# Third run of a four-step period in the order lists of an attention replaced by a list of its own to the attention's end

## The reference

```python
x = x + L0_xattn(ln(x), ctx)   # 16 heads of 128 in 4 groups, self and cross attention
x = x + L0_ffn(ln(x))          # 32 experts, top 8 of a softmax router, rerouted by similarity
x = x + L1_xattn(ln(x), ctx)   # latent attention with rotary parts and a mask
x = x + L1_ffn(ln(x))          # quantised gate, up and down projections
```

```python
q = ln(fp8_linear(ln_out, wq));  qx = ln(fp8_linear(ln_out, wqx))
k = ln(fp8_linear(ln_out, wk));  v = fp8_linear(ln_out, wv)
kx, vx = split(cond @ w_kv_x);   kx = ln(kx)
core = softmax(q k^T / sqrt(128)) v        # per batch and head, 256 x 256
xout = softmax(qx kx^T / sqrt(128)) vx     # per batch and head, 256 x 64
out = fp8_round(concat(core, xout) / proj_smooth) @ wproj.T * scale
```

## Time and profile before

| | before |
|---|---|
| median of three runs | 820.1 us (819.15 to 820.65) |
| profiled execution, own time | 821.01 us |
| its span | 819.2 us |
| PE busy | 776.4 us (95%) |
| DVE, ACT, POOL busy | 642.5, 538.4, 495.5 us |
| attention's last `project` (`add_o` follows) | 455.6 us |
| mean granted TensorE clock | 0.991 |

### The profile page before, as it was taken

How to read it: one execution, slowest core, us unless ns; L and a number is a source line. 1 busy time by engine, 2 the same in 40 slices (tenths; PEclk the granted TensorE clock), 3 DMA queues, 4 the chain that set the end, 5 groups by cost and what they waited for, 6 DMA issues and landing times.

```text
span 819.2 us, 14427 instructions
## 1 busy us (share of the span) xinstructions
PE 776.4 (95%) x4848; PEld 669.2 (82%) x4848; DVE 642.5 (78%) x1509; ACT 538.4 (66%) x1236; POOL 495.5 (60%) x858
## 2 busy tenths in 40 slices
PE   3678999999999999999899999999999999999997
PEld 2467888889888899888778878898888877777787
DVE  6878998989888898889889795766754658886644
ACT  6889878798787987788664555433332267986332
POOL 2698879997699976997856477424210125627410
PEclk9989999999999999999999999999999999999999
DMA  7000120012101030000200322977513000001001
GB/s 248 13 1 1 50 68 1 2 39 60 59 1 34 20 98 6 2 1 2 69 27 14 110 87 56 237 191 255 175 44 99 21 1 14 27 1 39 1 1 52
DMA packets 29224, 45.59 MB, mean 56 GB/s; under 512 B 4128, under 2 KB 18272, under 8 KB 29024
## 3 DMA queue, kind: packets, MB, share of 16 engines
q1 hardware_dynamic: 27760, 41.31, 17.0%
q10 hardware_dynamic: 1392, 3.37, 1.2%
HBM read 43.49 MB, written 1.18 MB: 55 GB/s over the span
## 4 chain that ended last, share of the span: by engine, by line
PE 81%; DVE 6%; ACT 6%; DMA 2%; issue 2%; POOL 2%; SPq 1%; ACTq 0%; DVEq 0%
PE PS L1077 17%; PE PS L937 10%; PE PS L1147 9%; PE PS L1032 6%; PE PS L968 6%; PE PS L1006 6%; PE PS L959 4%; PE PS L1261 3%; PE PS L978 3%; PE PS L989 3%; PE PS L1016 2%; PE PS L1213 2%; DMA l_S<-share 1%; PE PS L1223 1%; PE PS L1229 1%
## 5 line engine op out<-in xcount | busy, mean ns | idle before, releaser
L3240 POOL TENSOR_SCALAR raw<-raw,mvq,rsq 128x128 f32<-128x128 f32 x312 | 194.8, 638 | 1.6
L1077 PE MATMUL PS<-xq,WH 128*128 128x512 f32 x472 | 149.2, 397 | 0.0
L1077 PEld LDWEIGHTS PS<-xq,WH 128*128 128x128 f32 x472 | 86.3, 190 | 17.5 <-issue 1.9
L937 PE MATMUL PS<-WH,xq 128*128 128x256 f32 (+1 forms) x256 | 91.2, 373 | 9.9 <-DVE xq L2102 5.6
L1077 PE MATMUL PS<-xq,WL 128*128 128x512 f32 x236 | 92.9, 393 | 0.0
L937 PE MATMUL PS<-WL,xq 128*128 128x256 f32 (+1 forms) x256 | 83.3, 342 | 0.0
L2202 DVE BATCH_NORM_STATS2 st<-raw 128x6 f32<-128x128 f32 x320 | 75.3, 277 | 9.1 <-ACT raw L1398 7.7
L1147 PE MATMUL PS<-xq,m_hh 128*128 128x256 f32 x384 | 70.3, 283 | 2.0 <-ACT m_hh L1312 1.4
L1032 PE MATMUL PS<-PH,cat 128*128 128x256 f32 x256 | 67.8, 301 | 0.9 <-DVE cat L2102 0.9
L1426 ACT ACTIVATE P<-PS,sm 128x256 f32<-128x256 f32 x128 | 59.9, 483 | 13.1 <-DVE sm L2266 13.0
L1006 PE MATMUL PS<-PT,vr 128*128 128x256 f32 x256 | 66.3, 381 | 1.9 <-ACT kT L1415 1.4
(11 more groups left out here) (316 smaller groups left out, 2120.6 us busy)
## 6 DMA issues: line engine op xcount, KB each, us to landing
wst<-in_wgu SPq DMA_DIRECT2D x24, 256.0 KB, 2.9
wst<-in_wall SPq DMA_DIRECT2D x18, 256.0 KB, 3.1
l_KM<-share SPq DMA_DIRECT2D x9, 384.0 KB, 3.9
dst<-in_wdn SPq DMA_DIRECT2D x24, 128.0 KB, 2.6
wst<-in_wkvx SPq DMA_DIRECT2D x8, 256.0 KB, 3.4
m_pre<-in_wo ACTq DMA_DIRECT2D x1, 2048.0 KB, 11.7
l_KM<-share SPq DMA_DIRECT2D x6, 256.0 KB, 6.5
l_S<-share SPq DMA_DIRECT2D x6, 256.0 KB, 6.0
```

The costliest lines, as they stand in the source:

```text
L937: t = e.matmul(PS[:, b, o:o + n], xq[s][:, k, c * 128:(c + 1) * 128], W[:, k, w0:w0 + n], start=(k == 0 and i == 0), stop=(k == 1 and i == 1))
L1077: t = e.matmul(PS[:, b, :], W[wi][:, gu, k, :], a[:, k, cols], start=(n == 0), stop=(n == 5))
L3240: t = e.tensor_scalar(v, v, mvq[:, par, n, 0:1], rsq[:, par, n:n + 1], ALU.add, ALU.mult)
```

## The change

The loops of the period run twice instead of three times, and its `if g < 2` go. What the third run and the rule made is now a list of single calls on PE, ACT, DVE and POOL, with the same calls in another order. Four small pieces of code that stood between them got names (`split_gate`, `first`, `zero`, `turn_keys`) so that the lists can place them. Two waits moved into the functions that they guard: for `rounded` in POOL's `load_p` and in `load_gu`. The amount of work on each engine is as before.

```diff
 def attention_order(do):
-    for g in range(3):
+    for g in range(2):
...
-    units = [(s, k) for s in range(STEPS) for k in range(5)]
-    for n in range(BEGUN, len(units) + 5):
...
+    do("p1", 3, 7, 0)
+    do("project", 11, 2)
+    do("p1", 3, 6, 1)
+    do("p2", 14, 4)
...
+    do("project", 11, 3)
+    do("p2", 14, 0)
+    do("p1", 3, 7, 1)
+    do("values", 13, 0)
...
+    do("project", 12, 2)
+    do("project", 12, 3)
+    do("p2", 15, 4)
...
+    do("scores", 15, 2)
+    do("p2", 15, 3)
+    do("project", 13, 2)
+    do("xs", 0)
+    do("project", 13, 3)
+    do("values", 14, 3)
+    do("turn", 14, 4)
+    do("scores", 15, 3)
+    do("keys")
...
+    do("early", 0, 0)
+    do("project", 15, 0)
+    do("project", 15, 1)
+    do("early", 1, 0)
+    do("project", 15, 2)
+    do("project", 15, 3)
+    do("xs", 2)
+    do("logits", 1)
...
 def vector(e):
+            norm(14, 4)
+            split_x(0)
+            add_o(13)
+            maxima(15, 2)
+            split_gate()
+            ln_m(1)
...
 def gpsimd(e):
             def load_p(gp, p):
                 two = slice(2 * p, 2 * p + 2)
+                w.wait_ge(rounded.sem, rounded.at[12, 0])
...
+            norm_q(14, 5)
+            load_p(3, 2)
+            load_p(3, 3)
+            norm_q(14, 6)
+            norm_q(14, 7)
+            root_q(15)
...
+            norm_q(15, 7)
             norm_m(0)
+            load_gu(0)
+            zero()
+            load_gu(1)
             norm_m(1)
+            load_gu(2)
             load_dn(0)
             load_dn(1)
+            load_gu(3)
+            turn_keys()
```

More of the change, by code:

```diff
@@ L20 @@
 PARTS = (2, 0, 1)
-BEGUN = 73
 P2ORDER = (4, 0, 1, 2, 3)
@@ L310, in attention_order @@
         do("turn", 6 + 4 * g, 0)
-        if g < 2:
-            do("p1", 2 + g, 1, 1)
+        do("p1", 2 + g, 1, 1)
         do("p2", 7 + 4 * g, 0)
-    units = [(s, k) for s in range(STEPS) for k in range(5)]
-    for n in range(BEGUN, len(units) + 5):
[L316 to L350, removed]
@@ new lines, in attention_order @@
+    do("scores", 10, 3)
+    do("values", 10, 0)
+    do("turn", 10, 1)
+    do("p2", 11, 1)
+    do("kx", 3)
+    do("scores", 10, 4)
+    do("values", 10, 1)
+    do("turn", 10, 2)
+    do("p2", 11, 2)
+    do("p1", 3, 2, 2)
+    do("values", 10, 2)
+    do("turn", 10, 3)
+    do("scores", 11, 0)
+    do("p2", 11, 3)
+    do("p1", 3, 3, 2)
+    do("values", 10, 3)
+    do("scores", 11, 1)
+    do("turn", 10, 4)
+    do("project", 9, 0)
+    do("project", 9, 1)
+    do("p1", 3, 2, 0)
+    do("p1", 3, 3, 0)
@@ new lines, in attention_order @@
+    do("project", 9, 2)
+    do("scores", 11, 2)
+    do("p2", 12, 4)
+    do("scores", 11, 3)
+    do("values", 10, 4)
+    do("turn", 11, 0)
+    do("project", 9, 3)
+    do("p1", 3, 2, 1)
+    do("p1", 3, 3, 1)
+    do("p2", 12, 0)
+    do("values", 11, 0)
+    do("turn", 11, 1)
+    do("p1", 3, 4, 2)
+    do("scores", 11, 4)
+    do("p2", 12, 1)
+    do("values", 11, 1)
+    do("scores", 12, 0)
+    do("turn", 11, 2)
+    do("p2", 12, 2)
+    do("scores", 12, 1)
+    do("values", 11, 2)
+    do("turn", 11, 3)
@@ new lines, in attention_order @@
+    do("p2", 12, 3)
+    do("project", 10, 0)
+    do("p1", 3, 5, 2)
+    do("project", 10, 1)
+    do("p1", 3, 4, 0)
+    do("p1", 3, 5, 0)
+    do("values", 11, 3)
+    do("turn", 11, 4)
+    do("p1", 3, 4, 1)
+    do("project", 10, 2)
+    do("project", 10, 3)
+    do("p1", 3, 5, 1)
+    do("scores", 12, 2)
+    do("p2", 13, 4)
+    do("values", 11, 4)
+    do("scores", 12, 3)
+    do("turn", 12, 0)
+    do("p2", 13, 0)
+    do("kt", 3)
+    do("project", 11, 0)
+    do("values", 12, 0)
+    do("scores", 12, 4)
@@ new lines, in attention_order @@
+    do("scores", 14, 2)
+    do("turn", 13, 4)
+    do("project", 12, 2)
+    do("project", 12, 3)
+    do("p2", 15, 4)
+    do("scores", 14, 3)
+    do("values", 13, 4)
+    do("turn", 14, 0)
+    do("scores", 14, 4)
+    do("p2", 15, 0)
+    do("values", 14, 0)
+    do("turn", 14, 1)
+    do("project", 13, 0)
+    do("p2", 15, 1)
+    do("values", 14, 1)
+    do("scores", 15, 0)
+    do("turn", 14, 2)
+    do("p2", 15, 2)
+    do("project", 13, 1)
+    do("scores", 15, 1)
+    do("values", 14, 2)
@@ new lines, in attention_order @@
+    do("turn", 14, 3)
+    do("scores", 15, 2)
[7 more added lines that the diff above has]
+    do("keys")
+    do("values", 14, 4)
+    do("turn", 15, 0)
+    do("scores", 15, 4)
+    do("keys_r")
+    do("values", 15, 0)
+    do("turn", 15, 1)
+    do("logits", 0)
+    do("values", 15, 1)
+    do("turn", 15, 2)
+    do("project", 14, 0)
+    do("values", 15, 2)
+    do("turn", 15, 3)
@@ L353 @@
+    do("xs", 1)
+    do("project", 14, 1)
+    do("values", 15, 3)
+    do("turn", 15, 4)
+    do("project", 14, 2)
+    do("project", 14, 3)
+    do("values", 15, 4)
+    do("early", 0, 0)
[6 more added lines that the diff above has]
+    do("logits", 1)
 TAIL = 18
@@ L1751, in scalar @@
                 exps(6 + 4 * g, 2)
-                if g < 2:
-                    take_p1(2 + g, 0, 1)
+                take_p1(2 + g, 0, 1)
                 take_p2(7 + 4 * g, 0)
[L1755 to L1786, removed]
@@ L1788, in scalar @@
+            take_values(15, 4)
+            first(0)
+            first(1)
+            load_gu(3)
+            split_x(2)
             w.emptied(("o", STEPS - 1))
@@ L2772, in vector @@
+            go(y[30])
+            split_x(1)
+            go(y[30], 3)
+            add_o(14)
+            go(y[30])
+            go(y[31], 5)
+            ln_m(2)
+            add_o(15)
             w.emptied(("o", STEPS - 1))
```

558 lines of the change are left out of this document (462 added, 96 removed).

## The result

| | before | after |
|---|---|---|
| median | 820.1 us (5 runs, 819.0 to 820.78) | 814.5 us (5 runs, 811.53 to 816.26) |
| ratio after to before | | 0.9933, 95% interval 0.9908 to 0.9958 |
| profiled execution, span | 821.01, 819.2 us | 815.51, 813.7 us |
| PE idle from 388 to 446 us | 4.89 us | 0 |
| last values of the attention end | 444.63 | 438.52 |

The changed kernel is 5.6 us faster; 815.8 was forecast.

The account below looks back on a forecast made before the run. PE bounds up to 388 us; behind it order, not load, loses 7.1 us, 6.4 recoverable. Less 0.7 each for xs(0), xs(2) and small waits gives 4.3: median 815.8 from 820.1, range 813.8 to 819.3.

Parts of the forecast that it names:

- Up to 388 us: From 311 us PE has no wait to lose, so the new order brings 0, between -0.5 and +1 us of cost.
- wrong if PE waits in 311 to 388: Sign against the forecast: PE waiting between 311 and 388 us, a stretch that was to stay without a wait.
- The root of step 15: On POOL, it starts at 390.8 instead of 393.3, 2.5 us earlier, as its loads and seeds come sooner.
- project(12,2): PE's 0.9 us wait for `cat` goes: y[25] ends on DVE at 397.1, due about 397.8.
- `p2`(15,4): POOL's first pairs ready at 398.9, PE comes at 399.6; the waits for POOL, 1.3 us in sum, go.
- xs(0): xn ready at 416.1, PE there at 415.6: wait 0.5, with slower start 0.7, between 0 and 3 us.
- xs(2): Now directly behind project(15,3), PE waits between 0 and 0.9 us for ln_m(2); taken as 0.7.
- Small tenths: Less 0.7 us for waits left at tight places: project(12,2), the `l_KA` copy behind keys, turn(15,0).
- The gain carried to the end: From xs(2) on, router and experts do the same work behind the same logits, so the 4.3 us gain stays.
- The first rival: POOL's chain doesn't move, root at 393.3 or later; 1.2 to 2.5 us left, 817.6 to 818.9; chance 0.17.
- scores further ahead: Behind 388 us, 11.1 us of PE work instead of 6.2 from scores(15,4) to its transpose answers waits for `P` and ACT.
- about 0.9 shorter with none: POOL's root of step 15 runs about 0.9 us shorter if no DVE two-input instruction meets it, longer with one more.

Follow-up runs that it names:

- e2: Order of the kernel before up to about 388 us on PE, ACT, DVE and POOL, the changed kernel's order behind; 814.49 us beside 820.80, ratio 0.9933.
- e9: Changed kernel with DVE's last five seed steps for the root of step 15 moved behind maxima(13,4) alone; 817.26 us beside 820.34, ratio 0.9963.
- e5: Changed kernel with DVE's last five seed steps of step 15 behind maxima(13,4), a rounding pass and maxima(14,0); 820.19 us beside 820.48, ratio 1.0007.
- e3: Kernel before with transposes and values pushed one unit later behind unit 73, last roundings, projections and early halves too; 826.48 us beside 820.80, ratio 1.0095.
- e7: Kernel before with scores pulled one unit earlier on PE, exponentials on ACT, maxima and divisions on DVE; 822.65 us beside 820.48, ratio 1.0029.
- e6: Changed kernel's lists up to scores(15,0) at about 404 us (POOL's to the root of step 15), old order behind; 818.58 us beside 820.48, ratio 0.9970.
- e10: Changed kernel with DVE's five passes of each rounding y[26] to y[31] in one piece, nothing between them; 821.99 us beside 820.34, ratio 1.0018.
- e4: Order of the kernel before written as single calls in the changed kernel's code, with its moved waits for rounded; 820.37 us beside 820.80, ratio 0.9997.
- e11: Changed kernel with scores (15,1) to (15,4) one place later each on PE, exponentials, maxima and divisions moved along; 821.61 us beside 820.34, ratio 1.0008.
- e1: Changed kernel's lists up to about 388 us on all four engines, order of the kernel before behind; 820.01 us beside 820.80, ratio 0.9990.
- e8: Changed kernel with logits of batch 2 on PE ahead of the second early half instead of behind it; 817.07 us beside 820.48, ratio 0.9954.
- e12: Changed kernel with the router's group behind the sixth early half instead of the fifth, on PE and ACT; 813.39 us beside 820.34, ratio 0.9913.

## Why the prediction was right, and where its sizes were off

The mechanism was the one forecast: a loss of 7.1 us between 388.1 and 444.6 that no engine's load explains, 6.4 of it to be had by order, carried to the end. That the total came near (4.3 forecast, 5.6 measured) is in part luck: three deductions of 0.7 came to nearly nothing, and a term put at 0 cost 0.9. Its steps, with times of after as its trace has them (0.7 to be added beside before's and the forecast's):

- **Up to 388 us: mis-sized.** The 0 is 0.9 us of cost, inside the bounds that the forecast gave. PE idles 0.32 us of the 77 in after, for POOL's heads at `p2`(12,4), and 0.18 for an ACT copy at `p2`(11,1), the first call of the new order; before has neither wait. From turn(10,1) to the end of scores(13,4) PE takes 81.3 us, where before takes 77.3 and the moved work is worth 3.1. The sign "wrong if PE waits in 311 to 388" did come, by these tenths. With the old lists in front (e2) there is no wait, and 0.3 of the 0.9 are left.
- **The root of step 15.** Forecast 390.8 and 2.5 us earlier; measured 391.15, which is 391.8 in before's time and 1.5 us earlier. From it to xn 25.3 us were assumed, 24.3 measured: the root took 4.4 us to the first norming instead of 5.5, xn 1.1 instead of 1.6, the twenty normings 13.1 instead of 12.3.
- **project(12,2).** y[25] was to end at 397.1, due 397.8. Measured 397.81 and 397.87: just covered.
- **`p2`(15,4).** Ready 398.9 and due 399.6 in the forecast, 398.0 and 400.0 measured.
- **xs(0): mis-sized.** The term "less 0.7" is 0. In before's time xn came at 416.15, as forecast, and PE at 416.46 instead of 415.6: late by the 0.9 that it had lost before. The wait for xn, forecast as the longest, is none.
- **xs(2): mis-sized.** "I take 0.7" is 0 too. ln_m(2) ended at 447.58 and PE came at 448.0.
- **Small tenths: mis-sized.** "Less 0.7" is 0.1. From the end of scores(13,4) at 391.48 to values(15,4) at 438.52 PE takes 47.0 us for 46.3 of work, and 1.4% of that is the full stretch's own loss. Of the 6.4 us of an ideal order 5.4 were gained, and nearly all of the missing 1.0 was lost ahead of that point.
- **The gain carried to the end.** 5.4 us at values(15,4), 5.0 at the end of the logits, 4.8 at the end of the span, counted from turn(10,1). The slow stretch behind the logits was 6.8 us long in this execution instead of 3.4, 1.7 us more cost, but of the wait of 1.1 for DVE's chain only 0.3 was left. Over the runs the median gained 5.6.
- **The first rival's price.** "Root at 393.3 or later: 1.2 to 2.5 us are left." In before's time run e9 had it at 394.5 and kept 3.1 us, so the price is too high there; run e5 had it at 395.9 and kept nothing. I had no slow clock behind a long wait in it.
- **The reason "scores further ahead".** Right as a description of PE's list, wrong as a recipe: e3 and e7 did just that and were slower. What removes all waits at once is the set: scores early on PE, the seeds first on DVE, and DVE's roundings cut so that maxima and divisions come between the passes. Taking out any one of them cost 2.5 us or more of the 5.6 (e5, e6, e9, e10). The orders of ACT and of POOL behind 388 us were not tested by themselves.

## What to carry to other kernels

Where all engines wait a little and none is full, price the work, take the rest as loss, and expect one wait's removal to let in the next: here one wrong place on one engine lost half of the gain or all of it. A constant lag for all kinds of work is too blunt, since engines serve their lists in order; each engine's list has to follow the dates at which the others ask. Give a margin of a microsecond or two where a long chain meets the full engine, for a wait of 3 us there cost 5. Before a date of one trace is set beside that of another, measure how far apart the two stand at the last call that they share.

## What the runs showed of the hardware

- **The clock fell behind some of PE's waits and not behind others of the same length.** Waits of 1.93 us (e3), 2.69 (e6), 3.07 (e5) and 3.92 (e4) were followed by 3.4 us at 1.2 GHz each, and one of 3.67 (e11) by 5.6 us, with the last 1.2 us of the wait itself at that level. Waits of 1.63 (e9), 2.22 (e10), 2.69 (e7) and 2.72 us (e1) were not. So the length of the wait alone doesn't decide it.
- **The stretch behind the 32-column logits comes in some executions and not in others of the same order.** It is 3.4 us long in before, e2, e3, e5, e9 and e11, 6.8 in after, and missing in e1, e4, e6, e7, e8, e10 and e12; before and e4 have the same order. Part of the spread of the runs (811.5 to 816.3 for after) may be of this kind; it was not measured.
- **POOL's small steps depend on DVE's neighbours, and DVE's on POOL's.** In the root of step 15 in after, POOL's instructions on 20 numbers a lane take 0.21 to 0.23 us, but the one that starts at 392.98 takes 0.62, while DVE runs a conversion of two inputs (yb<-yT,fb) from 392.85 to 393.53. In e9 one takes 1.09 us, from 398.77, beside DVE's `cat` conversion from 398.53 to 399.77, and the next 0.70 beside a division. The other way round, DVE's two steps of 1.27 and 1.25 us in e2 stand beside POOL's loads. The Trainium skill says so in "SBUF — State Buffer", section "Who interferes with whom": of the two, one holds the other off for a whole instruction. The traces agree. The forecast's "about 0.9 shorter with none" was not put to the test as it stands: before had three long steps in the root (0.60, 0.56 and 1.09 us), after one (0.62), and the root was 1.2 us shorter.
